# One more partial sum on VectorE: seven product tiles instead of eight for the scalar messages of a graph layer

## The reference

```python
xs, xv = _split(x[col], 64, 32);  es, ev = _split(edge_attr, 8, 8)
s1 = einsum('ea,eb,abc->ec', xs, es, W1) / sqrt(64 * 8)
s2 = einsum('eai,ebi,abc->ec', xv, ev, W2) / (sqrt(3) * sqrt(32 * 8))
v1 = einsum('ea,ebi,abc->eci', xs, ev, W3) / sqrt(64 * 8)
v2 = einsum('eai,eb,abc->eci', xv, es, W4) / sqrt(32 * 8)
messages = concat([(s1 + s2) / sqrt(2), (v1 + v2) / sqrt(2)]) @ Wm + bm
agg = segment_sum(messages, row, num_segments=50000)
x = layernorm(x + x + concat([x, agg]) @ Wu + bu)
```

## Time and profile before

| | |
|---|---|
| time, median of 3 runs | 1928.71 us (1927.19 to 1929.68) |
| the profiled execution | 1923.78 us, of which span 1922.0 us |
| PE busy | 1660.2 us, 86% |
| VectorE busy | 1549.8 us, 81% |
| GpSimd busy | 1079.2 us, 56% |
| ScalarE busy | 894.5 us, 47% |
| mean data rate of the DMAs | 255 GB/s |

### The profile page before, as it was taken

One profiled execution on the slowest core, in us unless ns is written; L12 is line 12 of the kernel. 1 busy time (PEld: TensorE's weight loads), 2 busy tenths in 40 slices (PEclk: granted clock), 3 DMA queues, 4 the chain that ended last, 5 costly groups with the idle time before them and its releaser, 6 DMA issues.

```text
span 1922.0 us, 35044 instructions
## 1 busy us (share of the span) xinstructions
PE 1660.2 (86%) x11964; PEld 894.9 (47%) x11964; DVE 1549.8 (81%) x1727; ACT 894.5 (47%) x1721; POOL 1079.2 (56%) x837
## 2 busy tenths in 40 slices
PE   5439999999999999999999999999999999378883
PEld 2214444444444444444444444444444444266662
DVE  6347888888888888888888888888888886089994
ACT  1204444444444444444444444444444444168885
POOL 3106666766666666666666666666666665301110
PEclk9779999999999999999999999999999999789997
DMA  9996777777777777777777777777777774799994
GB/s 378 405 377 181 232 232 226 231 230 230 230 228 231 231 230 231 229 230 231 235 234 236 235 237 234 237 225 239 239 234 235 231 230 99 237 361 420 418 412 178
DMA packets 174616, 490.06 MB, mean 255 GB/s; under 512 B 48664, under 2 KB 99096, under 8 KB 149484
## 3 DMA queue, kind: packets, MB, share of 16 engines
q1 hardware_dynamic: 91980, 379.42, 51.6%
q0 software_dynamic: 82304, 109.12, 27.3%
q10 hardware_dynamic: 288, 0.95, 0.2%
HBM read 393.10 MB, written 96.31 MB: 255 GB/s over the span
## 4 chain that ended last, share of the span: by engine, by line
DMA 39%; issue 20%; POOL 20%; PE 11%; DVE 5%; ACT 2%; SPq 1%; POOLq 1%; ACTq 0%; DVEq 0%
DMA agg<-summed,row_idx 25%; POOL agg L324 14%; POOL xg L307 6%; DMA prod<-agg 5%; DMA xg<-in_x_rows,dst_sb 4%; DMA agg<-start_rows 4%; PE ps L648 3%; PE ps L641 2%; DVE stats L585 2%; DVE prod L566 2%; DMA e_sb<-in_e_rep 1%; ACT spread L365 1%; PE ps L694 1%; PE ps L629 1%; PE ps L695 1%
## 5 line engine op out<-in xcount | busy, mean ns | idle before, releaser
L324 POOL DMA_INDIRECT agg<-summed,row_idx x392 | 642.2, 1638 | 448.9 <-DMA agg<-summed,row_idx 294.0
L505 DVE TENSOR_TENSOR prod<-ps,e_sb 128x2048 f32<-128x2048 f32 x294 | 663.7, 2285 | 136.8 <-PE ps L648 132.2
L648 PE MATMUL ps<-prod,packed_sb 128*32 128x512 f32 x3136 | 752.7, 603 | 0.8 <-ACT S_sb L377 0.8
L307 POOL DMA_INDIRECT xg<-in_x_rows,dst_sb x392 | 410.5, 1047 | 179.4 <-issue 117.8
L641 PE MATMUL ps<-prod,packed_sb 128*32 128x512 f32 x2352 | 394.3, 600 | 0.0
L365 ACT ACTIVATE spread<-xg 128x1536 f32<-128x1536 f32 x98 | 145.5, 1485 | 424.1 <-DMA xg<-in_x_rows,dst_sb 413.5
L513 DVE TENSOR_TENSOR prod<-ps,e_sb 128x3072 f32<-128x3072 f32 x98 | 328.1, 3348 | 0.0
L493 DVE TENSOR_TENSOR prod<-ps,e_sb 128x2048 f32<-128x2048 f32 x98 | 223.9, 2285 | 108.6 <-ACT A_sb L371 69.4
L648 PEld LDWEIGHTS ps<-prod,packed_sb 128*32 128x32 f32 x3136 | 148.6, 109 | 156.7 <-issue 156.7
L629 PEld LDWEIGHTS ps<-packed_sb,spread 128*128 128x128 f32 x1176 | 127.3, 143 | 172.2 <-issue 123.6
L377 ACT ACTIVATE S_sb<-ps 128x512 f32<-128x512 f32 x98 | 58.7, 599 | 277.8 <-PE ps L648 277.8
(11 more groups left out here) (62 smaller groups left out, 1748.6 us busy)
## 6 DMA issues: line engine op xcount, KB each, us to landing
e_sb<-in_e_rep SPq DMA_DIRECT2D x98, 1536.0 KB, 7.2
e_sb<-in_e_rep SPq DMA_DIRECT2D x98, 1024.0 KB, 5.6
agg<-start_rows SPq DMA_DIRECT2D x49, 640.0 KB, 17.1
prod<-agg SPq DMA_DIRECT2D x48, 640.0 KB, 10.7
out<-prod POOLq DMA_DIRECT2D x48, 640.0 KB, 7.7
row_sb<-in_src_row SPq DMA_DIRECT2D x98, 256.0 KB
prod<-in_x_t SPq DMA_DIRECT2D x25, 640.0 KB, 11.8
e_sb<-in_x_t SPq DMA_DIRECT2D x24, 640.0 KB, 12.9
```

Of the source, the lines that this page charges most:

```text
L307: nc.gpsimd.indirect_dma_start(xg[g[1] % 2][:, q, :], None, x_rows, bass.IndirectOffsetOnAxis(dst_sb[g[1]][:, q:q + 1].bitcast(U32), 0)).t ...
L324: nc.gpsimd.indirect_dma_start(agg, bass.IndirectOffsetOnAxis(row_idx[g[1]][:, q:q + 1].bitcast(U32), 0), summed[g[1]][:, q // 2, q % 2 * ...
L505: nc.vector.tensor_tensor(prod[g[1] % 2][:, 4 + 4 * i:8 + 4 * i, :].rearrange("p (a b) e -> p a b e", b=2), ps[:, t_bank(g, 1 + i), :].uns ...
L648: return nc.tensor.matmul(ps[32 * quarter:32 * quarter + 32, S_BANK, :], w[:, 32 * half:32 * half + 32], prod[g[1] % 2][:, tile, :], start ...
```

## The change

A second sum on VectorE, after the third xv product, adds tile 14 onto tile 6 as well. PE then contracts seven tiles, 0 to 3, 6, 7 and 15, of which 15 keeps its own matmuls. The quarters 0, 1, 2 of the W2 round take tiles 3, 6, 7, and quarters 1 and 2 end there; `round_rest` does only tile 15, in quarters 0 and 3. `rounds` counts 7 steps a group, `parts_added` 2.

```diff
-ROUNDS = 8
+ROUNDS = 7
...
-            def add_parts(g):
-                dve.wait_ge(multiplied, number(g) * USES + 3)
-                total = prod[g[1] % 2][:, 6:8, :]
-                nc.vector.tensor_tensor(total, total, prod[g[1] % 2][:, 10:12, :], ALU.add).then_inc(parts_added, 1)
+            def add_parts(g, step):
+                dve.wait_ge(multiplied, number(g) * USES + 3 + step)
+                if step == 0:
+
+                    total, more = prod[g[1] % 2][:, 6:8, :], prod[g[1] % 2][:, 10:12, :]
+                else:
+
+                    dve.wait_ge(parts_added, number(g) * 2 + 1)
+                    total, more = prod[g[1] % 2][:, 6, :], prod[g[1] % 2][:, 14, :]
+                nc.vector.tensor_tensor(total, total, more, ALU.add).then_inc(parts_added, 1)
...
-                    add_parts(s)
+                    add_parts(s, 0)
                     times_xv(s, 2)
+                    add_parts(s, 1)
                     times_y(s)
...
-                tile = (0, 1, 2, 3, 6, 7, 14, 15)[k]
-                w = w1_sb[:, k, :] if k < 4 else w2_sb[:, k % 2, :]
+                tile = (0, 1, 2, 3, 6, 7, 15)[k]
+                w = w1_sb[:, k, :] if k < 4 else w2_sb[:, min(k - 4, 1), :]
...
-                pe.wait_ge(parts_added, number(g) + 1)
+                pe.wait_ge(parts_added, number(g) * 2 + 2)
                 for quarter in range(3):
-                    scalars(g, quarter, 3 + quarter, 1, stop=quarter == 2)
+                    scalars(g, quarter, 3 + quarter, 1, stop=quarter > 0)
...
             def round_rest(g):
                 scalars(g, 0, 6, 1, stop=True)
-                scalars(g, 1, 7, 1, stop=True)
-                scalars(g, 3, 6, 0).then_inc(rounds, 1)
-                scalars(g, 3, 7, 0, stop=True).then_inc(rounds, 1)
+                scalars(g, 3, 6, 0, stop=True).then_inc(rounds, 1)
```

## The result

The change made the kernel slower: 1976.1 us (median of 4 runs, 1968.8 to 1984.6) against 1928.0 us (4 runs); the ratio is 1.025, with an interval of 1.021 to 1.030. The forecast was 1922 us, faster, with a range from 1897 to 1947.

What follows compares the result with a forecast made beforehand. A two-slot loop through edge loads, scatter and gather landings and compute was taken to bound the kernel. Slots of 15.77 against 15.84 us over 86 slots gave -6 us, 1917.8 profiled; the median lies 4.9 higher, 1922, range 1897 to 1947.

Steps and rivals of the forecast that it cites:

- The loop and its legs: Loop over two slots: L217 load to scatter pair 6.92, to spreading 8.51, to L217 17.26 us; together 32.7 us.
- escapes: Scatter pairs starting some 3.5 us ahead of L217 load, next pair soon after; claimed mostly lost, one in ten slots.
- Part (1): PE's rest round: two of four passes go, 0.86 us off the leg from spreading to L217, 17.26 to 16.4.
- (5): Head and tail of the kernel: PE done some 2.6 us earlier only lets node loads start earlier; taken as 0.
- Part (2): VectorE's new sum: 0.73 us a slot, off the 17.26 us leg and covered by VectorE's waits for PE.
- Part (3): L221 load (vector edge features) 4.0 us behind L217, not 3.27; effect between -0.2 and +0.73 us a loop, taken as 0.
- first leg: From the issue of L217 to the scatter pair on the path, caught in edge-load traffic: 6.92 us.
- gather leg: From the scatter pair on the path, over a gather's second half, to ScalarE's spreading: 8.51 us.
- Rival C: Later L221 moves a landing on the path by 0.5 to 0.73 us: slower, 1947 to 1956 us, chance 0.16.
- Part (4): GpSimd's calls held by the new sum, whose inputs are both in SBUF: about 0.1 us a slot, taken as 0.

Runs made afterwards that it cites:

- pe_alone: Kernel before with only PE's part of the change: tile 14 neither added nor contracted, rest round of two passes; 1913.3 us, ratio 0.990.
- before_last: Kernel before with its one sum of 1024 columns moved behind the y product; 1896.4 us, ratio 0.984.
- port_after_y: Kernel before plus a sum of 512 columns, two SBUF inputs, unread result, behind the y product; 1929.7 us, ratio 1.000.
- sum_last: The changed kernel with its second sum behind the y product instead of ahead of it; 1909.7 us, ratio 0.990.
- hold_there: As late_full, but the added instruction between third xv product and y product is a sum of two SBUF inputs; 1958.0 us, ratio 1.015.
- late_full: sum_last plus an unread product of 720 columns that reads PSUM, between third xv product and y product; 1955.8 us.
- late_vectors: Kernel before plus an unread product of 512 columns that reads PSUM, between third xv product and y product; 1964.4 us, ratio 1.018.
- deep_before: Kernel before with four buffers of gathered rows instead of two and each gather issued one slot earlier; 1930.2 us.
- same_last: sum_last with PE's summing matmuls moved behind the y and rest rounds; 1933.2 us.
- together: sum_last with the L217 load held until the y product is done too, so L217 and L221 go out together; 1971.0 us.
- late_third: sum_last plus an unread product of 128 columns that reads PSUM, between third xv product and y product; 1927.5 us, ratio 0.998.

## Why the prediction was wrong

- **The loop and its legs** were read rightly from the trace of before: 17.26 became 16.34 us. Half the three legs gives 16.20 us a slot before, 15.65 in pe_alone and 15.42 in before_last, against 15.73 and 15.52 measured there, so shortening the leg on PE or on VectorE does shorten the loop by half of it. The kernel before itself runs at 15.85, below its 16.20, thanks to its escapes; they are lost with the shorter leg, and so only part of the gain is seen against it. What I had not seen is that GpSimd never gets ahead however many buffers it has.
- **Part (1)**, 0.86 us of PE per slot: measured 0.92 on the leg. Alone, it gives slots of 15.73 us where 15.77 was forecast, and 1913.3 us, where the forecast, which took parts (2) to (5) at nothing, had 1922. The escapes were lost as forecast.
- **Part (2)**: the sum takes 0.69 us, L221 comes 0.82 later (0.73 forecast). VectorE's time was covered (port_after_y).
- **Part (3) is the step that failed.** I weighed L221's delay between -0.2 and +0.73 us per loop and took 0, looking only at the gather on the path, which lands when the DMA engines are at a third of their share. sum_last and the change differ in nothing but the place of the second sum, and between them the first leg goes from 6.85 to 7.38 us and the gather leg from 8.01 to 8.39: 0.91 us per loop of two slots, more than my upper bound. (Against the kernel before the gather leg looks unchanged, 8.44 and 8.39, because the shorter leg on PE alone had brought it to 8.05.) The pair behind the one on the path comes 8.15 us after it in place of 6.80, and so falls later with respect to the next L217: 30 times within 1.6 us behind it, once in sum_last and never before. There it delays the first leg, and where it starts 0.9 us or more behind, the next pair comes 11 to 12 us later and slots of 20 to 24 us follow. The 0.46 us a slot of the legs, 39 us over 86 slots, and some 33 us of long slots come to 72 us; the medians of the two kernels differ by 66 us, their profiled executions by 75. Rival C named the cause and priced it at 1947 to 1956; it was 1976.
- **Part (4)** was right to be 0: holding GpSimd is real, but in the change it adds up to 32.5 us against 35.0 before, and it costs nothing measurable in hold_there. The Trainium skill (SBUF — State Buffer, Who interferes with whom) has a GpSimd instruction that reads SBUF wait in full for a VectorE one with two SBUF inputs that was issued first, and infers that the generation of descriptors is not held by such a sum. The traces go with the rule and against the inference: calls that start within a sum take up to 2.62 us where others take 1.59.
- **Left open**: why the change has more of the slots of 20 to 24 us than late_full and hold_there with the same L221, worth about 18 us.

## What to carry to other kernels

Ask of an added instruction not only whether its engine has time, but which release on its engine comes later by it; here 0.6 us on an edge load's release cost 36 us (late_vectors) and 0.8 us cost 66 (the change against sum_last), and standing behind that release cost nothing. When waits are for DMA landings, look at how transfers fall between each other, and put whatever releases nobody last in the slot. And a stall seen over a whole slot moves by more than the delay: go by the pair that comes next, not only by the one on the path.

## What was not expected of the hardware

The same program can fall into a better pattern by itself. One of 11 executions of the kernel before in one job took 1855.9 us, the others 1924.8 to 1937.0, and one of deep_before took 1880.9 where the others took 1926.6 to 1935.5. The profiled execution of same_last changed pattern in its course: 17 slots from 1291.1 us on take 14.95 us each, 67 before that 16.07.

```profile
L493 DVE TENSOR_TENSOR prod<-ps,e_sb x18: 2278/2284/2285, 1291.1 to 1545.3; 128x2048 f32<-128x2048 f32 x18
...
L493 DVE TENSOR_TENSOR prod<-ps,e_sb x68: 2277/2284/2293, 199.2 to 1276.2; 128x2048 f32<-128x2048 f32 x68
```

In the fast part all but one of 34 pairs start 6.9 to 7.6 or 13.7 to 14.7 us behind an L217. What makes an execution fall into it wasn't tried. The change also spreads more from run to run (1968.8 to 1984.6) than the kernel before, as do late_full and together. And one of ten executions of late_third took 4729 us, which no trace explains.
